# A gated relational GNN layer: x and the first weight land first, POOL's scattering DMAs make the edge table, and DVE alone runs the last stage on three buffers

## What is computed

```python
h = relu(layernorm(x))
u = h @ root + bias
for r in range(8):
    mask = (edge_type == r)
    sums = segment_sum(h[src] * mask[:, None], dst)
    cnt  = segment_sum(mask, dst)
    u = u + (sums / maximum(cnt, 1)[:, None]) @ weight[r]
z = concatenate([u, h]) @ w_gate + b_gate
out = x + tanh(u) * z + h * (1 - z)
```

## Time and profile before

| | us |
|---|---|
| median of 3 runs | 1543.31 |
| lowest and highest | 1542.98, 1546.41 |
| profiled execution, its own time | 1540.62 |
| its span | 1538.9 |
| mean granted clock of PE | 0.978 |

### The profile page before, as it was taken

One profiled execution on the slowest core, in us unless ns is written; L12 is line 12 of the kernel. 1 busy time (PEld: TensorE's weight loads), 2 busy tenths in 40 slices (PEclk: granted clock), 3 DMA queues, 4 the chain that ended last, 5 costly groups with the idle time before them and its releaser, 6 DMA issues.

```text
span 1538.9 us, 21083 instructions
## 1 busy us (share of the span) xinstructions
PE 1431.4 (93%) x6978; PEld 770.1 (50%) x6978; DVE 668.3 (43%) x1167; ACT 340.8 (22%) x419; POOL 645.1 (42%) x1021
## 2 busy tenths in 40 slices
PE   1998897889899998999999999999999999999897
PEld 1444443456555544554545544455454456566564
DVE  4577758555552242224323312422432343456534
ACT  4544121101110211022121102212112220323221
POOL 2411000779772445434435444444443454530343
PEclk9999999899999999999999999999999999999999
DMA  5621411030015433734643463374455346532665
GB/s 201 242 93 66 160 43 42 14 134 1 1 39 195 127 120 109 240 113 146 212 155 121 132 227 127 113 244 135 127 175 202 123 149 228 158 90 63 175 195 152
DMA packets 63441, 207.40 MB, mean 135 GB/s; under 512 B 12709, under 2 KB 13084, under 8 KB 63354
## 3 DMA queue, kind: packets, MB, share of 16 engines
q1 hardware_dynamic: 34554, 122.15, 22.7%
q0 software_dynamic: 28224, 81.95, 18.3%
q10 hardware_dynamic: 576, 2.10, 0.4%
HBM read 170.67 MB, written 56.32 MB: 148 GB/s over the span
## 4 chain that ended last, share of the span: by engine, by line
PE 81%; DVE 7%; DMA 4%; issue 3%; ACT 2%; POOL 1%; SPq 0%; POOLq 0%; DVEq 0%; ACTq 0%
PE ps L947 66%; PE ps L890 10%; DMA reg<-y_rows,idx 3%; PE ps L878 2%; PE ps L880 1%; DVE u L617 1%; DVE W L605 1%; DMA ints<-in_src_dram 1%; DVE u L613 1%; ACT yhl L521 1%; POOL reg L349 1%; PE ps L921 1%; DVE yhl L694 0%; DMA W<-in_x_dram 0%; ACT reg L451 0%
## 5 line engine op out<-in xcount | busy, mean ns | idle before, releaser
L947 PE MATMUL ps<-W,hT 128*128 128x512 f16 (+2 forms) x5280 | 1193.0, 383 | 0.1
L947 PEld LDWEIGHTS ps<-W,hT 128*128 128x128 f16 (+2 forms) x5280 | 580.3, 111 | 542.8 <-issue 19.7
L374 POOL DMA_INDIRECT reg<-y_rows,idx x196 | 220.3, 1124 | 155.8 <-POOL idx L371 128.2
L694 DVE SCALAR_TENSOR_TENSOR yhl<-ps,yhl 128x1024 f16<-128x1024 f32 x80 | 97.9, 1224 | 421.8 <-ACT yhl L521 421.8
L521 ACT ACTIVATE yhl<-ps 128x1024 f16<-128x1024 f32 x80 | 81.8, 1023 | 792.2 <-PE ps L947 792.2
L349 POOL TENSOR_SCALAR reg<-iota_t,ework 125x128 f16<-125x128 f16 x160 | 144.4, 910 | 163.3 <-DVE inv L667 130.6
L890 PE MATMUL ps<-reg,onehot 128*125 x784 | 193.5, 387 | 18.5 <-POOL onehot L381 14.6
L381 POOL TENSOR_SCALAR onehot<-iota_d,dcol 128x125 f16<-128x125 f16 x180 | 115.0, 639 | 102.2 <-DMA reg<-y_rows,idx 96.5
L370 POOL COPY dcol<-edge_dst 128x1 f32 x196 | 46.9, 239 | 238.2 <-PE ps L893 231.8
L890 PEld LDWEIGHTS ps<-reg,onehot 128*125 x784 | 99.8, 138 | 74.8 <-issue 24.2
L440 ACT ACTIVATE W<-W,wsc 128x1024 f16<-128x1024 f32 x88 | 96.5, 1140 | 89.8 <-PE ps L947 79.8
(11 more groups left out here) (128 smaller groups left out, 626.1 us busy)
## 6 DMA issues: line engine op xcount, KB each, us to landing
y_rows<-yhl SPq DMA_DIRECT2D x72, 512.0 KB, 3.0
W<-in_L_gnn_weight_dram SPq DMA_DIRECT2D x60, 512.0 KB, 11.4
W<-in_L_gnn_w_gate_dram SPq DMA_DIRECT2D x16, 512.0 KB, 13.2
reg<-in_x_dram SPq DMA_DIRECT2D x9, 512.0 KB, 4.3
hs_rows<-reg SPq DMA_DIRECT2D x9, 512.0 KB, 5.1
zh_rows<-reg SPq DMA_DIRECT2D x10, 448.0 KB
W<-zh_rows SPq DMA_DIRECT2D x10, 448.0 KB
W<-hs_rows SPq DMA_DIRECT2D x10, 448.0 KB
```

The lines of the kernel that those rows point to most:

```text
L374: pool.indirect_dma_start(out=G[:, b, :], out_offset=None, in_=y_rows[rel], in_offset=bass.IndirectOffsetOnAxis(ap=idx[:, b, :], axis=0), ...
L694: nc.vector.scalar_tensor_tensor(out=yhl[0:rows, m % 2, D:2 * D], in0=whole, scalar=2.0 ** -Y_BITS, in1=yhl[0:rows, m % 2, 0:D], op0=ALU.mult,
L947: last = nc.tensor.matmul(ps[0:rows, b + half, :], hT[:, v_h, k, n0:n0 + rows], Wh[:, HOME[w][k], v_w, half * HC:(half + 1) * HC], start=( ...
```

## The change

**Order at the start.** x tiles 0 and 1 are loaded first, then all eight pieces of the first weight, all from SP, then the edge arrays; ACT issues no loads any more. `LEAD` is 2 and not 3. `edge_keys` runs on DVE in the iteration of slot 1. The second weight's loads wait for `wtop_ready`.

**Edge table.** The table steps on PE, DVE and POOL go. DVE computes, with each quarter of the positions, each edge's address in a table in HBM and src*128 + dst packed in one integer (`places`). POOL issues 160 indirect DMAs that each write 125 integers of 4 bytes to `table_rows`, loads the table back, and DVE unpacks it after slot 38 (`LOAD_AT`). The first groups are summed from half slot 79 on and not 59; the last ten stay, so there is one in 1.49 half slots between.

**Gathers.** The two small copies that a gather needs (`dcol`, `idx`) are made one gather earlier (`columns`).

**Last stage.** POOL and ACT do none of it but tanh. DVE prepares x + h and zh * (tanh(u) - h) before the product is done, with four operations, and needs two after it. Three buffers each. The last slot's matmuls run one half of the columns after the other, and DVE and the store follow in halves.

```diff
-    AGG_FROM, AGG_LAST = 2 * 29 + 1, 2 * slot(W_GH, 1) + 1
+    AGG_FROM, AGG_LAST = 2 * 39 + 1, 2 * slot(W_GH, 1) + 1
...
-    LEAD = 3
+    LEAD = 2
...
+    LOAD_AT = slot(3, 8)
...
+    NZ = 3
...
             load_x(0)
-            land(0, 0, 2)
             load_x(1)
-            land(0, 2, 4)
+            land(0, 0, KT)
...
-            for c in range(EC):
-                if c >= NBUF:
-                    pool.wait_ge(s["step_used"], c - NBUF + 1)
-                low_source(c, c % NBUF)
+            pool.wait_ge(s["table_filled"], 16)
+            for c in range(EC):
+                if c % (EC // SQ) == 0:
+                    pool.wait_ge(s["pos_ready"], c // (EC // SQ) + 1)
+                pool.indirect_dma_start(out=table_rows, out_offset=bass.IndirectOffsetOnAxis(ap=at_i[:, c:c + 1], axis=0),
+                                        in_=packed[:, c:c + 1], in_offset=None).then_inc(s[f"scattered{c // (EC // SQ)}"], 16)
+            for b in range(SQ):
+                pool.wait_ge(s[f"scattered{b}"], 16 * EC // SQ)
+            pool.dma_start(table_i[:, :], table_rows.rearrange("(p t) one -> p (t one)", p=P)).then_inc(s["table_loaded"], 16)
...
+            def columns(t, b):
+
+                pool.wait_ge(s["tile_ready"], t + 1)
+                pool.reg_alu(last_row, last_row, N - 1, ALU.min)
+                pool.tensor_copy(dcol[:, b, :], edge_dst[:, bass.ds(t, 1)]).then_inc(s["idx_ready"], 1)
+                pool.tensor_copy(idx[:, b, :], edge_src[:, bass.ds(t, 1)]).then_inc(s["idx_ready"], 1)
+
             def gather(rel, q, b):
                 t = pool.snap(q * RING + b)
+                columns(pool.snap(t + 1), (b + 1) % RING)
                 pool.wait_ge(s["onehot_free"], t + 1)
-                pool.tensor_copy(dcol[:, b, :], edge_dst[:, bass.ds(t, 1)]).then_inc(s["idx_ready"], 1)
-                pool.tensor_copy(idx[:, b, :], edge_src[:, bass.ds(t, 1)]).then_inc(s["idx_ready"], 1)
...
             def table():
-                dve.wait_ge(s["step_used"], EC)
-                nc.vector.tensor_copy(edge_dst[:, :], ps[:, 5, 0:TMAX])
-                step(nc.vector.tensor_scalar(iota_t[:, :], ps[:, 5, 0:TMAX], 0.0, 2.0 * P * 8, ALU.is_equal, ALU.mult))
-                nc.vector.tensor_tensor(edge_src[:, :], ps[:, 4, 0:TMAX], iota_t[:, :], ALU.add).then_inc(s["table_ready"], 1)
+                dve.wait_ge(s["table_loaded"], 16)
+                step(nc.vector.tensor_scalar(edge_src[:, :], table_i[:, :], 7, None, ALU.logical_shift_right))
+                step(nc.vector.tensor_scalar(table_i[:, :], table_i[:, :], P - 1, None, ALU.bitwise_and))
+                nc.vector.tensor_copy(edge_dst[:, :], table_i[:, :]).then_inc(s["table_ready"], 1)
...
-            edge_keys()
...
+                    if w == 0 and j == 1:
+                        edge_keys()
...
+                        prepare_tile(j)
+                        if j == NJ - 1:
+                            dve.wait_ge(s["first_half"], 1)
+                            finish_tile(j, 0, HC)
+                        dve.wait_ge(s["gemm_done"], t + 1)
+                        finish_tile(j, HC if j == NJ - 1 else 0, D)
```

More of the change, by code:

```diff
@@ L163, in gated_rgcn_preln @@
         src_f, dst_f, typ_f, grp, dst1, key, pos, hi_t = (ework[0:EP, b * EC:(b + 1) * EC] for b in range(8))
[L164 to L174, removed]
+        at_f = typ_f
+        at_i, packed, spare_i = (ints[0:EP, b, :] for b in range(3))
+        zslot = [i for i in range(NSLOT) if i not in HOME[W_GU]]
+        zh_in, h_in, x_in = ([W[:, zslot[NZ * v + b], :] for b in range(NZ)] for v in range(3))
         s = {n: sem(n) for n in (
@@ new lines, in finish_tile @@
+            def finish_tile(j, c0, c1):
+                rows = DTL[j][1]
+                b = 2 * (slot(W_GU, j) % 2)
+                part = ps[0:rows, b:b + 2, :].rearrange("p b n -> p (b n)")[:, c0:c1]
+                nc.vector.scalar_tensor_tensor(out=zh_in[j % NZ][0:rows, c0:c1], in0=part, scalar=zsc[0:rows, j:j + 1],
+                                               in1=u[0:rows, j, c0:c1], op0=ALU.mult, op1=ALU.mult).then_inc(
+                                                   s["evac"] if c1 == D else s["dve_step"], 1)
+                if c1 == D:
+                    dve.wait_ge(s["evac"], slot(W_GU, j) + 1)
+                else:
+                    steps[0] += 1
+                    dve.wait_ge(s["dve_step"], steps[0])
+                nc.vector.tensor_tensor(zh_in[j % NZ][0:rows, c0:c1], zh_in[j % NZ][0:rows, c0:c1], x_in[j % NZ][0:rows, c0:c1],
@@ L779, in _ @@
                     t = slot(w, j)
-                    if t >= STEP0 and t < STEP0 + NJ:
-                        for c in range((t - STEP0) * STEP_TILE, (t - STEP0 + 1) * STEP_TILE):
-                            table_step(c)
                     if RANK0 <= t:
@@ L941, in _ @@
                     b = 2 * (t % 2)
+                    if t == NW * NJ - 1:
+                        for half in range(2):
+                            for k in range(KT):
+                                for v_h, v_w in ((0, 0), (0, 1), (1, 0)):
+                                    last = nc.tensor.matmul(ps[0:rows, b + half, :], hT[:, v_h, k, n0:n0 + rows],
+                                                            Wh[:, HOME[w][k], v_w, half * HC:(half + 1) * HC],
+                                                            start=(k == 0 and v_h + v_w == 0), stop=(k == KT - 1 and v_h == 1))
+                            last.then_inc(s["gemm_done"] if half else s["first_half"], 1)
+                        break
                     for k in range(KT):
@@ L954, in _ @@
                             rank_chunk(ch)
-                        if STEP0 <= t < STEP0 + NJ:
-                            for c in range(2):
-                                table_step((t - STEP0) * STEP_TILE + k * 2 + c)
                         if k == 3:
```

180 lines of the change are left out of this document (75 added, 105 removed).

## The result

| | us |
|---|---|
| changed kernel, median of 4 runs | 1476.08 (1475.25 to 1476.63) |
| kernel before, beside it | 1543.25 |
| ratio to before, 95% interval | 0.956 (0.954 to 0.958) |
| predicted | 1445.0 (1427 to 1465) |
| profiled execution's span, mean granted clock | 1474.3, 0.979 |

The kernel is 67 us faster and not 98. The time lies 11 us above the top of the range: 31 us were promised and did not come.

A forecast was written before the change was run, and what follows sets the result against it. PE, busy 93% of the span, was taken to bound the kernel. Terms 84.7 + 2 + 8 + 0.5 + 3 = 98.2 us off the median 1543.3 gave 1445.1 us, range 1427 to 1465.

The forecast's parts named there:

- the table steps: Slots 17 to 26: without the one-hot table work on PE's path, ten slots of 10.38 us remain, 84.7 us less.
- "nothing" in slots 13 to 16: Seven small DVE operations behind each quarter, some 1.3 us a slot, were to cost no time.
- 1.12 us of POOL: Edge table: each of 160 scattering DMAs takes POOL as long as a gather, 180 us in all, ending at 415.
- the limit of 1.54: Edge table: POOL may take 247 us for 160 DMAs, 1.54 us each, before DVE asks for the table at 487.
- 67 early: Edge table: the scatters were to end at 415, 67 us early for DVE's request.
- The second rival: Table comes late, each DMA over 1.54 us: 1518 us at 2.0 us a DMA, 1838 at 4.0; chance 9%.
- 125 packets: Scattering DMAs: 0.16 us a packet, so 1.25 us a DMA over 16 engines, 4.0 with only five.
- I take 8 us off: Sums of messages: earlier column copies shorten POOL's turn, denser groups have room; 8 us less (bounds plus 5 to 20 less).
- The third rival: Sums of messages: PE waits for DVE's add or a gather in denser groups, 20 us, 1465 in all; chance 7%.
- The start: First product 14.6 us earlier, mostly lost to longer waits ahead of slots 4 to 9; slot 10 only 2 us earlier.
- The last stage: End of the kernel: two half operations and half the last store save 3 us, the stage's start 0.5.

The follow-up runs named there:

- e11: Kernel e7 with gathers of 2 KB a row and not 4, half of each row of G left as it was: 1440.28 us against 1452.54.
- e7: The changed kernel with both edits of e1 and e5: 1452.54 us, ratio 0.940 to the kernel before.
- e1: The changed kernel with the table read one slot later and the sums begun from half slot 83: 1457.85 us, ratio 0.9445 to the kernel before.
- e5: The changed kernel with the copies of hT ahead of the next tile's statistics (DVE) and normalisation (ACT): 1466.80 us, ratio 0.9514 to the kernel before.
- e6: The changed kernel with 64 addresses a scattering DMA and not 125, edges of 61 partitions left out: scatter pace 1.20 us, from 1.49; no total time given.
- e10: The changed kernel with 100 addresses a scattering DMA and not 125, edges of 25 partitions left out: 1649.73 us in its one, disturbed execution.
- e12: The kernel of e10 once more, now timed without the profiler too: 1461.25 and 1465.10 us.
- e2: The kernel before with one number changed, the sums of messages from half slot 79 on and not 59: 1559.46 us, ratio 1.0098.
- e4: The kernel before with the change's start alone (order of loads, LEAD 2, edge keys at slot 1): 1543.66 us, ratio 1.000.

## Why the prediction was wrong

**The sum.** Right: the view that PE bounds the kernel, and the table steps, 84.6 us where 84.7 stood. What was called "nothing" in slots 13 to 16 cost nothing.

**The step that failed first: "1.12 us of POOL" a scatter.** The likeness with the gather was good for the instruction, 1.19 against 1.12, and that bytes are not POOL's work e11 bears out, where a gather of half the bytes keeps it busy 1.09 us and e7's 1.08. The step took the instruction's length for its pace. In the gathers' rows something else always stands between two of them; 160 in a row show 0.30 us from each to the next, and four pauses ahead of the 40th, 80th, 120th and 160th (7.24, 3.56, 3.61 and 4.10 us from start to start, against 1.49). They stand at the same four places in e1, e5, e7 and e11 and not in e6, e10 or e12. 254 us for 159 steps are 1.60 a DMA, past the limit of 1.54 that the prediction itself had worked out. The table missed DVE by 8 us, where the sum had it 67 early: 59 of the 76 us between are the pace (1.49 for 1.12), 12.5 the four pauses, the rest a few longer DMAs. By this sum the table would have come at about 484 without the pauses, ahead of DVE's question at 488.4; that is an estimate, no run takes them away alone at 125 addresses.

The second rival described this and priced it wrongly. It counted only DVE's wait. At 1.60 it would have given (1.60 - 1.54) x 160 = 10 us; e1 gives 18 back. Behind DVE's unpacking stand POOL's column copies, a gather that lands in 9.0 us beside the weight's eight loads, and a one-hot matrix, 16 us from 496.55 on, where the kernel leaves PE one slot of work, 10.4 us, between the unpacking's place and the first sum. e6, whose table is early (DVE doesn't wait for it), takes 10.1 us from there to the first sum and still shows PE waiting 2.0, 1.2, 1.4, 1.7 and 4.4 us for the first five tiles, so one slot is short even then. The first of them, in e6:

```profile
498.61 1.05 PE L889 MATMUL ps<-reg,onehot 128*125 x4 [1.97 <-POOL onehot L398]
```

The prediction never asked how long it is from the table to the first sum.

The bound from the other side, "125 packets" at 0.16 us each, 1.25 us a DMA on 16 engines and 4.0 on five, was mis-sized too. The trace has 32 packets a DMA, 1.8 us of packet time for all engines together, where 125 x 0.16 would be 20. So the packets were not what set the pace of 1.49; POOL's instruction and the gap behind it make it up. What the four pauses wait for stays open. Issue to landing is 2.6 us for 125 addresses, 2.2 for 100 and 2.0 for 64, POOL's own 1.19, 0.99 and 0.89 within it, which leaves 1.4, 1.2 and 1.1. On the number of engines, before the run nothing showed how a DMA of 125 addresses is spread. The Trainium skill (DMA: Bandwidth & Descriptors, "Why a DMA increments its semaphore by 16 and not by 1") gives five engines for 125, ten for 100 and sixteen for 64, and a cursor by which POOL's DMAs go on to the next ones. The packets agree with the division in their size: 25, 10 and 4 numbers are 125, 100 and 64 by five, ten and sixteen, and an even spread of 125 over 16 would be 8. The trace doesn't show which engine took a packet, and it has 16 of this size in every case, so no run here shows the number of engines or the cursor; and since what is left of the landing, 1.4 us, is shorter than the pace, the transfers need not overlap.

**The second step that failed: "I take 8 us off".** It was two terms in one, with the sign of the sum from the wrong one. The earlier copies gave 12 (the term was sized 20 at most, fairly). The denser groups were argued to cost nothing, "4 us a tile, which POOL's 2.2 and the transfer of 0.5 MB have room in": a mean over all groups, while a transfer alone takes 4.6 us from issue to landing (median of the changed kernel) and several tiles follow at once. They cost 15. The third rival had this price (20) with two causes, and e2 and e11 show the one, gathers, and not DVE's add. Together with the late table: 3 + 18 = 21 of the 24.2 us in the table above. The other 3 are within what two executions differ by: in e1's profile the stretch from slot 27 to slot 103 takes 1015.5 us, 20.5 less than in the changed kernel's.

**The start.** The mechanism was right: first product at 27.9 (26.2 said), waits of 6.9, 7.9, 9.3 and 1.8 us ahead of slots 4, 6, 8 and 9 (7, 8, 9 and 2 said), the first three with a slow spell behind them. Only the size of the gain was off, 13 us and not 14.6 at the front and so +0.7 and not -2 at slot 10. By e4 the whole start is worth nothing.

**The last stage.** Right in its parts, 5 us and not 3.5; from DVE's last read of PSUM to the end it gave 4.7 where 3 were said.

**The range** held the uncertainty of the single terms and one rival at a time. Here two came together, the late table and the denser groups, and both raise the time. The three smaller misses of the sum, +2.7 at the start, +0.1 at the table steps and -1.9 at the last stage, nearly cancel by chance.

## What to carry to other kernels

Before work is moved to another engine's queue, multiply by the pace of a long run of it, not by the length of a single row, and lay the whole chain from its last instruction to the first consumer beside the work that has to cover it. A margin worked out to the third figure (1.54 against 1.12) deserves the question what the same instruction does 160 times in a row. Packing consumers closer to make room for a producer has a price of its own where they refill from a short ring of buffers; test it alone, as e2 did, since it can eat what another edit gains.

## What the runs showed of the hardware

- In a row of scattering DMAs POOL never starts the next less than 0.30 us behind the end of the one before, at 64, 100 and 125 addresses alike; busy time is 0.89, 0.99 and 1.19 us.
- 125, 100 and 64 scattered numbers of 4 bytes go in 32 packets a DMA each time, 16 of them with 25, 10 and 4 numbers; such a packet takes 0.114, 0.018 and 0.011 us.
- In a row of 160 with 125 addresses POOL pauses ahead of every 40th, 2 to 6 us, in five kernels of five; with 64 or 100 addresses (three kernels) it doesn't. The cause was not tested.
- Two starts of the same product stage that differ by 13 us can end within 1 us of each other (e4), since the waits that follow are set by DVE's scans and ACT's copies, and behind the longer ones the granted clock is at its lower level for a few us (0.50 from 148.1 to 151.8 in the changed kernel).
